# Layer 1's experts as blocks of 32 sorted tokens, held stationary in column tiles of TensorE, 16 of them with fixed experts

## The reference, cut to what matters

```python
logits = hidden @ router_w.T                       # 16 experts
top_vals, top_idx = jax.lax.top_k(logits, 1)
scores = sigmoid(top score at its expert, -inf elsewhere)
routed_in = hidden[None] * scores.T[:, :, None]
gate, up = split(einsum('nth,nhf->ntf', routed_in, gate_up_proj))   # 128 -> 2 x 128
routed_out = einsum('ntf,nfh->nth', up * silu(gate), down_proj)     # 128 -> 128
shared = silu(hidden @ shared_gate_w.T) * (hidden @ shared_up_w.T) @ shared_down_w.T
return shared + routed_out.sum(axis=0)
```

## Time and profile before

| | |
|---|---|
| median of three runs | 1884.55 us (1883.86 to 1889.12) |
| the profiled execution | 1885.66 us, its span 1883.9 us |
| busy share of the span | PE 86%, PEld 49%, DVE 67%, ACT 54%, POOL 42% |
| granted TensorE clock, mean | 0.928 |
| chain that ended last, by engine | PE 57%, DVE 22%, ACT 9%, POOL 6%, issue 5% |
| DMA | 105.40 MB, 56 GB/s over the span |

### The profile page before, as it was taken

One profiled execution on the slowest core, in us unless ns is written; L12 is line 12 of the kernel. 1 busy time (PEld: TensorE's weight loads), 2 busy tenths in 40 slices (PEclk: granted clock), 3 DMA queues, 4 the chain that ended last, 5 costly groups with the idle time before them and its releaser, 6 DMA issues.

```text
span 1883.9 us, 29013 instructions
## 1 busy us (share of the span) xinstructions
PE 1617.2 (86%) x10660; PEld 923.8 (49%) x10660; DVE 1266.4 (67%) x2849; ACT 1023.9 (54%) x1967; POOL 797.6 (42%) x734
## 2 busy tenths in 40 slices
PE   6889999867988899987798899998779898999867
PEld 3557664312555666431255567643135456764214
DVE  4655648998554465699855455489976455558995
ACT  4465436654546444666555544376545554446654
POOL 2231225786232121478614221268951422026992
PEclk9989999878999999998899999899889999989878
DMA  6004402020000440202000054021200005402110
GB/s 223 1 1 135 139 16 73 29 90 7 18 1 1 139 132 19 73 29 90 12 12 1 1 150 124 16 74 51 68 12 6 1 3 157 120 16 90 45 52 11
DMA packets 91981, 105.40 MB, mean 56 GB/s; under 512 B 7104, under 2 KB 70336, under 8 KB 91584
## 3 DMA queue, kind: packets, MB, share of 16 engines
q1 hardware_dynamic: 89792, 99.37, 17.2%
q0 software_dynamic: 2048, 4.20, 0.7%
HBM read 80.60 MB, written 22.94 MB: 55 GB/s over the span
## 4 chain that ended last, share of the span: by engine, by line
PE 57%; DVE 22%; ACT 9%; POOL 6%; issue 5%; DMA 1%; DVEq 0%; SPq 0%; ACTq 0%; POOLq 0%
PE P L238 10%; DVE M L2038 8%; PE P L1652 5%; PE P L1881 4%; POOL M L2108 3%; PE P L406 2%; PE P L1233 2%; PE P L2166 2%; PE P L1238 2%; PE P L1828 2%; PE P L1249 2%; PE P L220 2%; PE P L978 1%; DVE M L200 1%; PE P L1205 1%
## 5 line engine op out<-in xcount | busy, mean ns | idle before, releaser
L2038 DVE TENSOR_TENSOR_SCAN M<-P,M 128x512 f32<-128x512 f32 x384 | 442.9, 1202 | 16.2 <-ACT P L1973 13.3
L1973 ACT ACTIVATE P<-M,negA 128x512 f32<-128x512 f32 x384 | 262.8, 689 | 171.0 <-DVE M L2038 170.2
L238 PEld LDWEIGHTS P<-wt,M 128*128 128x128 f32 x2176 | 275.0, 194 | 98.7 <-issue 34.6
L1881 PE MATMUL P<-M,wt 32*32 32x512 f32 x3072 | 242.9, 708 | 87.1 <-DVE M L2038 63.8
L238 PE MATMUL P<-wt,M 128*128 128x128 f32 x2176 | 292.6, 281 | 13.2 <-DVE M L2074 5.1
L2108 POOL TENSOR_TENSOR M<-M 128x512 f32<-128x512 f32 x192 | 238.5, 1275 | 97.6 <-ACT M L1955 73.7
L2108 POOL TENSOR_TENSOR M<-W,M 128x512 f32<-128x512 f32 x192 | 246.1, 1314 | 52.8 <-PE P L1881 52.7
L1881 PEld LDWEIGHTS P<-M,wt 32*32 32x32 f32 x3072 | 39.7, 111 | 244.1 <-DVE M L2038 169.8
L1652 PE MATMUL P<-M,wt 128*128 128x512 f32 x256 | 133.1, 602 | 0.3 <-ACT M L1701 0.2
L1749 DVE TENSOR_TENSOR M<-M,P 128x512 f32<-128x512 f32 x128 | 86.1, 679 | 69.1 <-PE P L1660 68.7
L1701 ACT ACTIVATE M<-P 128x512 f32<-128x512 f32 x128 | 75.8, 592 | 79.3 <-PE P L1652 78.9
(11 more groups left out here) (352 smaller groups left out, 3253.7 us busy)
## 6 DMA issues: line engine op xcount, KB each, us to landing
W<-in_e SPq DMA_DIRECT2D x88, 192.0 KB, 2.6
M<-in_e SPq DMA_DIRECT2D x64, 192.0 KB, 2.7
M<-dt SPq DMA_DIRECT2D x48, 256.0 KB, 4.7
M<-xs SPq DMA_DIRECT2D x32, 256.0 KB, 3.1
ys<-M SPq DMA_DIRECT2D x32, 256.0 KB, 2.4
W<-du SPq DMA_DIRECT2D x32, 256.0 KB, 4.9
W<-xh SPq DMA_DIRECT2D x16, 256.0 KB
M<-du SPq DMA_DIRECT2D x16, 256.0 KB, 4.9
```

The source lines that it names most:

```text
L238: m = e.matmul(out[:, tok(j)], h[:, tok(j)], wgt, start=first and j == 0, stop=last, skip_group_check=True)
L1881: m = e.matmul(t["sums"][i // 2][to:to + 32, :], part("WC", c)[r, r], scan[r, :], start=c == 0, stop=c == 5, tile_position=(32 * i, to))
L1973: e.activation(t["aa"][n % 2][:, :], t["dtr"][i][:, :], EXP, scale=negA[:, c:c + 1]).then_inc(ACT.s, ACT.mark(b, "a3", "aa", n))
L2038: e.tensor_tensor_scan(bb[:, :], t["aa"][n % 2][:, :], bb[:, :], 0.0, MUL, ADD).then_inc(DVE.s, DVE.mark(b, "a3", "scan", n))
```

## The change

- Blocks have 32 tokens. The first 16 blocks (`f1_first`) belong to experts 0 to 15, one each, and need no number. What an expert has beyond 32 tokens goes to one of at most 512/32 - 1 = 15 more blocks (`NMORE`, `f1_more`), whose expert is read from `eb`. So there are 31 blocks and two halves, `v` = 0 (the 16 fixed) and `v` = 1 (the 15 others; a sixteenth repeats the last one's work).
- The tokens are now stationary: 32 tokens are 32 columns, and the block's weights move past them, gate and up together (256 columns, L1254 of the new code), then down (128 columns, L1276). Four blocks stand in the four column tiles of the array. The hidden values have to be turned between the two (`turn_h`, L1263): 4 + 4 transposes of 128x128 more; the tokens themselves need 8 (L1239) in place of 19.
- The fixed experts' weights are fetched early, without a number: eight in one DMA when the lane's previous a3 is done, eight in two DMAs when the lane's own a1 has read its last features (`qkv`). The 15 others are fetched by number: five when `eb` is there, three behind the two loads of sorted tokens, seven when the shared expert's last `up` is done. In all 31 fetches' worth of 192 KB in place of 19.
- ACT has 10 instructions for the blocks (6 of 512 columns, 4 of 256) in place of 15, DVE 8 of 256 columns in place of 10 of 512.
- The ranking has 3 more DVE instructions, and two of them are larger (`need` has 16x15 elements, not 16x4); `eb` is now computed ahead of `pos`.
- `TURNS` is new for all engines.

```diff
@@
-NBLK = T // 128 + NEXP - 1
+NMORE = T // 32 - 1
+NROW = 32 * (NEXP + NMORE + 1)
@@
+        def f1_first(L, k):
+            at = 22 * T + 384 * (k - 8) if k < 13 else 18 * T + 384 * (k - 13)
+            return L.W[:, 384 * k:384 * k + 384] if k < 8 else L.M[:, at:at + 384]
+        def f1_more(L, d):
+            if d == NMORE - 1:
+                return L.X[:, :]
+            at = 12 * T + 384 * d if d < 8 else 6 * T + 384 * (d - 8) if d < 10 else (T, 20 * T + 128, XT * T, 0)[d - 10]
             return L.M[:, at:at + 384]
...
@@ pe_ffn1
-                for i, k in enumerate(GROUPS[g]):
-                    m = e.matmul(P[2][:, tok(i)], f1_weights(b, g, i)[:, 0:128], xsT[g % 2][:, tok(i)], start=True, stop=True)
...
+            def gate_up(v, i):
+                yield
+                if v == 0:
+                    w.wait_ge(firsts_in[s], 48 * (b // 2 + 1))
+                    w.wait_ge(DVE.s, DVE.of(b, "f1", "h" if i else "sw", 3))
+                else:
+                    w.wait_ge(more_in[s][i], 16 * (8 - i) * (b // 2 + 1))
+                    w.wait_ge(DVE.s, DVE.of(b, "f1", "gated", 0, i))
+                w.wait_ge(ACT.s, ACT.of(b, "f1", "xsT", v))
+                for g in (2 * i, 2 * i + 1):
+                    for k in range(4):
+                        r = slice(32 * k, 32 * k + 32)
+                        m = e.matmul(P[2 + i][r, 256 * (g % 2):256 * (g % 2) + 256], xsT[v][:, 128 * g + 32 * k:128 * g + 32 * k + 32],
+                                     f1_weights(L, v, g, k)[:, 0:256], start=True, stop=True, tile_position=(0, 32 * k))
...
+            yield from turn(0)
+            yield from gate_up(0, 0)
+            yield from gate_up(0, 1)
+            yield from turn(1)
+            yield from turn_h(0)
+            yield from gate_up(1, 0)
+            yield from gate_up(1, 1)
+            yield from down(0)
+            yield from turn_h(1)
+            yield from down(1)
...
@@ sp_ffn1
+            yield
+            w.wait_ge(PE.s, PE.of(b, "a1", "qkv", 1))
+            fetch_firsts(e, b, L.M[:, 22 * T:22 * T + 5 * 384], 8, 13)
+            fetch_firsts(e, b, L.M[:, 18 * T:18 * T + 3 * 384], 13, 16)
             yield
             w.wait_ge(DVE.s, DVE.of(b, "f1", "eb"))
+            fetch_more(0, 5)
+            yield
+            w.wait_ge(tokens_out[s], 64 * (b // 2 + 1))
+            for v in range(2):
+                e.dma_start(v3(sorted_x[v][:, :], 4), rows(xs_d[s], v)).then_inc(sorted_in[s][v], 16)
+            fetch_more(5, 8)
+            yield
+            w.wait_ge(PE.s, PE.of(b, "f1", "up", 3))
+            fetch_more(8, NMORE)
+            for v in range(2):
+                yield
+                w.wait_ge(ACT.s, ACT.of(b, "f1", "y", v))
+                e.dma_start(rows(y_d[s], v), v3(y[v][:, :], 4)).then_inc(y_out[s][v], 16)
...
@@ sp_attn0
+            yield
+            if b > 1:
+                w.wait_ge(PE.s, PE.of(b - 2, "a3", "y"))
+            fetch_firsts(e, b, lanes[b % 2].W[:, :], 0, 8)
```

More of the change, by code:

```diff
@@ L1241, in expert_out, with turn @@
-            def expert_out(g):
-                yield
-                w.wait_ge(DVE.s, DVE.of(b, "f1", "h", g + 4))
-                if g == 0:
-                    w.wait_ge(DVE.s, DVE.of(b, "f1", "x0"))
-                else:
-                    w.wait_ge(ACT.s, ACT.of(b, "f1", "y", g - 1))
-                for i, k in enumerate(GROUPS[g]):
-                    m = e.matmul(P[0][:, tok(i)], h[g % 2][:, tok(i)], f1_weights(b, g, i)[:, 256:384], start=True, stop=True)
-                m.then_inc(PE.s, PE.mark(b, "f1", "down", g))
+            def turn(v):
+                yield
+                w.wait_ge(sorted_in[s][v], 16 * (b // 2 + 1))
+                if v:
+                    w.wait_ge(ACT.s, ACT.of(b, "f1", "xsT", 0))
+                else:
+                    w.wait_ge(DVE.s, DVE.of(b, "f1", "pos"))
+                for g in range(4):
+                    m = e.transpose(P[1][:, tok(g)], sorted_x[v][:, tok(g)], ident)
+                m.then_inc(PE.s, PE.mark(b, "f1", "xsT", v))
@@ new lines, in turn_h, with down @@
+            def turn_h(v):
+                yield
+                w.wait_ge(ACT.s, ACT.of(b, "f1", "hT", 0) if v else ACT.of(b, "f1", "xsT", 1))
+                w.wait_ge(DVE.s, DVE.of(b, "f1", "gated", v, 1))
+                for g in range(4):
+                    m = e.transpose(P[1][:, tok(g)], h[v][:, tok(g)], ident)
+                m.then_inc(PE.s, PE.mark(b, "f1", "hT", v))
+            def down(v):
+                yield
+                if v:
+                    w.wait_ge(ACT.s, ACT.of(b, "f1", "y", 0))
+                else:
+                    w.wait_ge(DVE.s, DVE.of(b, "f1", "x0"))
+                w.wait_ge(ACT.s, ACT.of(b, "f1", "hT", v))
+                for g in range(4):
+                    for k in range(4):
+                        r = slice(32 * k, 32 * k + 32)
+                        m = e.matmul(P[0][r, tok(g)], hT[v][:, 128 * g + 32 * k:128 * g + 32 * k + 32],
+                                     f1_weights(L, v, g, k)[:, 256:384], start=True, stop=True, tile_position=(0, 32 * k))
+                m.then_inc(PE.s, PE.mark(b, "f1", "down", v))
@@ L1275, in pe_ffn1 @@
             yield from shared_out(3)
-            yield
-            w.wait_ge(DVE.s, DVE.of(b, "f1", "eb"))
-            turn(0)
-            for g in range(len(GROUPS)):
-                yield from expert(g)
-                if g:
-                    yield from expert_out(g - 1)
-                if g + 1 < len(GROUPS):
-                    yield
-                    turn(g + 1)
-            yield from expert_out(len(GROUPS) - 1)
+            yield from turn(0)
+            yield from gate_up(0, 0)
@@ L1428, in dve_ffn1 @@
             e.tensor_tensor(x, x, P[0][:, :], ADD).then_inc(DVE.s, DVE.mark(b, "f1", "x0"))
[L1429 to L1433 removed]
+            for v in range(2):
+                for i in range(2):
+                    yield from expert_gated(v, i)
             yield
+            w.wait_ge(DVE.s, DVE.of(b, "f1", "x0"))
             w.wait_ge(tokens_back[b % 2], 64 * (b // 2 + 1))
[L1436 removed]
             e.tensor_tensor(x, x, back[:, :], ADD).then_inc(DVE.s, DVE.mark(b, "f1", "x"))
         def pool_ffn1(e, w, b):
[L1440 removed]
+            L, sorted_x, xsT, th, h, hT, y, back = f1_tiles(b)
             xk = L.T[XT]
```

275 lines of the change are left out of this document (123 added, 152 removed).

## The result

| | before | after |
|---|---|---|
| median | 1886.84 us (1883.86 to 1891.09) | 1824.72 us (1823.67 to 1828.14) |
| ratio, 95% interval | | 0.967 (0.965 to 0.969) |
| span of the profiled execution | 1883.9 us | 1826.3 us |
| granted TensorE clock, mean | 0.928 | 0.931 |

The kernel is 62 us faster by the medians and 57.6 us by the profiled spans. The forecast was 42 us less, 1842.5.

What follows compares the result with a forecast made beforehand. PE's program was taken to bound f1's surroundings. Lane 0's 6.5 us plus lane 1's 5 made 11.5 a pair, 46 over four, 42 less a tenth: 1885.7 - 42 - 1.1 = 1842.5 us, range 1818 to 1870.

Steps and rivals of the forecast that it cites:

- PE's work after: PE in f1: six calls at 1.0 us plus 16 transposes, 7.8 us a batch in place of 14.8.
- two streams only: Rival, 4%: f1's column-tile calls cost L978's price, 3 us lost, 6 us of waits won back, about 1882 us.
- The term for the tiling changes: PE in f1: six excursions into column tiles at 0.14 us each, 0.8 us a batch, inside the calls' 6.0.
- The waits of lane 0: Lane 0's f1: later `pos` idles PE about 1 us, `gate_up(1, 1)` waits 1 to 1.5; net 6.5 us earlier.
- Times four: Whole kernel: 11.5 us a pair gives 46 us over four pairs, less a tenth: 42 us.
- In f1's surroundings PE's program is the bound: Eight stretches with f1, PE busy 665 of 722 us: work taken out shortens them unless a wait replaces it.
- a3 stays as long as it is and begins earlier: Stretch a3, DVE busy 153 of 160 us: length untouched by the change, only its start moves earlier.
- The fetch by number paces f1: Rival, 16%: late landings or later `pos` cost each f1 2 us more; 26 us gained in all, 1858 us.
- More is won: Rival, 12%: cheaper PE calls, covered waits, ACT and DVE relieved in f1; 8 us a batch, 64 us, 1821 us.
- The neighbours swallow it: Rival, 5%: the other lane holds the last stages before a3, half of each pair's gain is lost; 1872 us.
- The wait lets the clock fall: Rival, 5%: PE's wait at `gate_up(1, 1)` drops its clock, 3.7 us more; 2.2 us lost per batch, 1902 us.
- A store behind the early fetch: Rival, 3%: lane 0's stores queue behind lane 1's eight early experts on SP, 20 us in all, 1862 us.

Runs made afterwards that it cites:

- after_twice: The changed kernel with every `gate_up` and `down` matmul issued twice over the same output: 1851.26 us, 0.983 of before.
- after_same_tile: The changed kernel with the loops of `gate_up` and `down` turned, column tile outer and block inner: 1843.83 us, 0.976 of before.
- before_half: The kernel before with two of the four blocks in each group left out on PE (gate, up, down): 1865.49 us, 0.990 of before.
- after_old_a3: The changed kernel with the old order of steps in a3, f3 and the next a0 alone: 1844.64 us, 0.978 of before.
- after_no_numbers: The changed kernel with the 15 extra blocks' weights fetched from fixed places, without the choice by number: 1815.05 us, 0.963 of before.
- after_seven_first: The changed kernel with seven fetches by number, not five, ahead of the wait for sorted tokens and one behind the loads: 1814.43 us, 0.964 of before.
- after_all_by_number: The changed kernel with no early fetch; the 16 fixed experts fetched singly behind `eb`, each after reading a number: 1905.85 us, 1.010 of before.

## Why the prediction was right, and where it was not

**PE's work after: right.** The forecast priced the new form by L1009, 1.0 us for either call; measured are 0.89 to 1.0 and 1.01, so a batch costs 4 x 0.93 + 2 x 1.0 + 1.8 = 7.5 us in place of 7.8. The "two streams only" rival is out. The term for the tiling changes was right in size too: 0.08 to 0.11 us (0.97 or 1.0 against 0.89) where 0.14 stood; there are four of them in lane 0's f1 of the second pair (at 615.79, 619.78, 624.25 and 628.55), not six, since some calls follow each other. Sixteen passes of 256 columns would be 32 x 0.11 = 3.5 us at the price of the whole array's passes; 0.89 is four times less. The Trainium skill (TensorEngine Tiling (Array Packing), Theoretical Speedup) gives up to 4x for 32 columns: the trace agrees for `gate_up` (4.0) and comes short of it for `down` (3.5), which stands alone between two tiling changes; a second `down` issued behind the first adds only 0.87 us in after_twice. L978's price, 2.2 times L1009's by column, did not carry over.

**The waits of lane 0: right, step by step, in the pair that was read.** Counted from `eb`: the first turn was forecast 12.2 us behind it and came 12.16 behind (600.98 to 613.14); the fifteenth fetch landed 23.2 behind where 23.8 stood; PE reached `gate_up(1, 1)` 9.95 us behind the first turn where 10 stood, and waited 1.16 us, 1.5 in the mean of lane 0's four batches, where 1 to 1.5 stood. In lane 1, where up to 1.8 stood, it did not wait. `eb` came 2.1 us behind `need` where it had been 2.7, so 0.6 us earlier in place of 0.4; `pos` came 3.2 us behind it, not 3.7, so it moved back by 1.5 us in place of 1.8; a fetch took 1.16 us of SP, not 1.1; the landings took 2.5 to 2.6 us in the median, 2.6 to 2.7 before. In this pair lane 0's f1, from the end of a1 to the end of f1, went from 62.8 to 55.3 us (7.5 less; 6.5 forecast) and lane 1's from 66.2 to 62.1 (4.1; 4.5 to 5 forecast). The sum of the two, 11.6, is the forecast's 11.5. That the sum fits is in part luck: in the other three pairs the same sum is 15.7, 27.1 and 20.4 us, while the stretch got only 4.9, 8.1 and 7.3 us shorter. The two f1 overlap, and their lengths do not add up to time.

**Times four: the mis-sized term.** That pair was not like the others. It had the longest f1 stretch before, 191.7 us against 175.8 to 179.8, and it gained 16.4 us there, lane 1's neighbours included; the other three gained 4.9, 8.1 and 7.3. Together 36.7, where 46 stood before the tenth was taken off. The prediction read its timeline in one pair and multiplied. What stands behind the number is the share of PE's relief that reaches the time: 37 us of 8 x 7.3 = 58, that is 0.63, where 42 of 56 (0.75) was forecast. Two runs give the same share by another way: 0.6 of the work that after_twice adds shows, and of the 2.7 us a batch that after_same_tile adds 0.6 to 0.9. before_half, with 0.4, gives less. The rest goes into waits: PE's idling in the eight stretches grew by 20 us.

**"In f1's surroundings PE's program is the bound": half of it.** before_half takes 48 us of PE's work away and 20 show, none in the first pair of its trace; idle time and the lower clock take the rest. In lane 0 of the second pair the fetches by number were exactly as late as PE, which the 1.44 us of idling had shown in the prediction's own first part. That the change works because it does both (four fewer numbers with five of them ahead of the tokens, and 7.3 us less work) is likely but not shown: the fetches alone bring nothing, the work alone 20 us, and the old kernel with both was not run.

**"a3 stays as long as it is and begins earlier": wrong.** This is the step that failed, though the number came out inside the range. a3, f3 and what follows to the next f0 are 19 us shorter over the whole span, and the new numbers in `TURNS`, which the prediction costed at nothing outside f1, are the reason for most of it. The runs give it from both sides: 15 to 21 us are lost if a3, f3 and a0 go back to the old order, 28 to 30 if all does, and 10 us are won by the new order alone in the kernel before. With after_old_a3 as the kernel of which the forecast spoke (new f1, old a3), its 42 us stand against 38 to 42 measured. But that close agreement owes something to the rest of the order as well: with the old order everywhere outside f1, 28 to 30 us are left. Two errors of opposite sign are in the forecast: too much for the relief, nothing for the order. That they partly cancel is luck. What the gain in a3 consists of is shown only for the first pair, where the old order lets PE stand 7.90 us for a DVE step and DVE's scans come 8.8 us later; the lower clock (0.89 against 0.93 in that stretch) goes with it, but most of it falls behind 390, where a3's delay no longer grows.

**The rivals.** *The fetch by number paces f1* left 26 us of gain, 1858, which did not come; but as a mechanism it is there, in lane 0, and is worth 9 us (after_no_numbers, after_seven_first). *More is won* names the right side for the wrong reason: f1 gave less, not more. *The neighbours swallow it*: no stage before a3 gave back half; in part it is what the 0.63 says. *The wait lets the clock fall*: in the first trace it did not, at waits of 0.5 to 2.4 us; the passes behind them ran at full speed (0.84 us for ten). In the second trace it did once: behind a wait of 2.08 us, which ended at 1521.01, the granted clock was 0.50 for 3.4 us, and a `down` took 1.89 us; behind one of 3.27 us, at 171.38, the passes ran at full speed. In after_all_by_number PE stands up to 13 us at a time; behind a wait of 12.25 us (641.92) four transposes took 1.11 us in place of 0.60, and the mean clock of the whole is 0.917. *A store behind the early fetch*: with 1.5 MB of early fetches issued at 622.37, y's first store, issued at 626.88, took 3.65 us to land, where the first one of that place took 2.97 before. The median of the sixteen stores is 2.3 us, 2.4 before: the loss did not come.

**What stays open.** Which steps of the order carry the gain, and whether it is the order itself or the place at which the lanes meet that lets a3 run, is not told apart: the smallest piece tried was a3, f3 and a0 together. The kernel before with all of the new order was not tried, since its f1 has other steps; nor was the kernel before with both its fetches and its PE work relieved. All orders here were made by hand for one kernel and taken to the other as they stood; how much an order made anew for the kernel before would bring it is not known.

## What to carry to other kernels

When an order by hand comes with the change, price it by itself: take the new order, as far as it fits, to the old kernel, and the old one to the new; here it was half of the gain, and a third of that was open without the change. Do not count on an engine's relief in full where two lanes share it (0.4 to 0.6 of it showed here), look for the second resource that is as late as the first, and read more than one period of the loop before multiplying. Where a fetch needs a number, ask which part of the data is needed whatever the number says, and fetch that first; then fill the queue's idle time ahead of its next wait.

## What the runs showed that I had not expected

- Column tiles lose nothing when two blocks in a row (four passes of 256 columns) go to the same tile: 0.89 us, as when the calls go round all four. With four blocks in a row on one tile (eight passes of 128 columns) `down` took 2.36 us in place of 1.01.
- Reading a number and issuing a fetch by it costs SP 1.1 to 1.16 us; a fetch from a fixed place behind a number that is read and not used costs 0.92 to 0.98 (eight in 7.21 and in 6.79 us, the last issue itself taking a third of a us).
- Adding 42 us of PE work cost 25 to 27 us, taking 48 away brought 20. Neither is the whole, and they need not be alike: added work first fills waits, and work that is taken away uncovers them and leaves PE more of its time at the lower clock (58.0 us in place of 37.5 in before_half's four stretches).
- Half speed on PE cost nothing where DVE had no idle time: the changed kernel's two traces had PE at the lower clock for 23.9 and for 17 us between 388 and 415 us, and DVE's scans came at the same distances.
